# Second cross attention of a two-layer decoder: dense queries and 64-row score matmuls, one head per half of the rows and per bank

## The chip, the core and the metric

The kernel runs on one core of a Trainium2 chip. A core has five engines that run side by side and tell each other by semaphores how far they are: TensorE (PE: matmuls, with weight loads that the trace lists apart as PEld), VectorE (DVE), ScalarE (ACT), GpSimd (POOL) and SyncE (SP), which here issues the DMAs. Matmuls write to PSUM, eight banks of 128 partitions by 512 float32 numbers. The metric is the device time of one execution in microseconds. TensorE's clock is granted by a throttle at one of two levels; the traces show it as 1.00 (2.4 GHz) or 0.50 (1.2 GHz), or a mean of the two.

## The reference, cut to the stage of the change

Six sublayers follow each other, each with a residual and a layer norm: self attention, cross attention, experts, then the same three again in other forms. The change is in the fifth.

```python
def _L1_xattn_ref(query, context, w_q, w_kv, w_out, b_out):
    # NUM_HEADS 16, HEAD_DIM 64, B 8, 128 queries of width 128, 120 context rows of width 96
    q = query @ w_q
    kv = context @ w_kv
    k, v = jnp.split(kv, 2, axis=-1)
    q = q.reshape(B, NQ, NUM_HEADS, HEAD_DIM).transpose(0, 2, 1, 3)
    k = k.reshape(B, NKV, NUM_HEADS, HEAD_DIM).transpose(0, 2, 1, 3)
    v = v.reshape(B, NKV, NUM_HEADS, HEAD_DIM).transpose(0, 2, 1, 3)
    scores = jnp.einsum('bhqd,bhkd->bhqk', q, k) * SCALE
    attn = jax.nn.softmax(scores, axis=-1)
    out = jnp.einsum('bhqk,bhkd->bhqd', attn, v)
    out = out.transpose(0, 2, 1, 3).reshape(B, NQ, INNER)
    return out @ w_out + b_out

x = _layernorm(x + _L1_attn_ref(x, ...), axis=-1)
x = _layernorm(x + _L1_xattn_ref(x, ctx_768, ...), axis=-1)
x = _layernorm(x + _L1_ffn_ref(x, ...), axis=-1)
```

## The kernel before, in words

Every engine has its own program, written out in the order in which it runs; nothing is reordered by a scheduler, and the engines meet only at semaphores (`wait_ge`, `then_inc`).

The 16 heads are 64 wide, so two heads fill 128 partitions, and the stage works on 8 such pairs. The activations stand transposed in `xT` (128 features by 1024 tokens, 8 batches of 128), the context in `ctxT` (96 by 960, 8 batches of 120). For pair `n`, in the buffers of `slot` n modulo 2:

- TensorE projects the queries (`project_queries`, L872, two matmuls of 512 tokens into banks 0 and 1), ScalarE and VectorE copy them out and scale them. Head j = 0 of the pair lies in partitions 0 to 63, head 1 in 64 to 127. ScalarE copies partitions 0 to 63 and VectorE 64 to 127 into `qz`, which has two 128-column blocks a batch: in block 0 the partitions of head 1 are zero, in block 1 those of head 0. GpSimd writes these zeros once, with the memsets of L549 and L551, ahead of the stage.
- Keys (L880, copied by ScalarE into `kE`) and values (L888, copied by ScalarE into `vE`), in the same banks 0 and 1.
- Scores (`pair_scores`, L899): 16 matmuls of 128 rows by 120 columns, in four groups `g` of four. A group covers two batches and both heads, goes to one of two banks (2 and 3, in turn), and waits for VectorE to be through with the group two before it. The zeros in `qz` let a matmul over all 128 partitions give the scores of one head.
- VectorE takes a group's maximum (L1595) and subtracts it (L1597) into `probs`, ScalarE takes the exponential (`pair_exps`), VectorE sums and inverts (L1607, L1608), GpSimd multiplies (L559).
- TensorE transposes the probabilities (`pair_weights`, L909, four groups, banks 4 and 5 in turn), ScalarE copies each group into `ptE`; then come the value matmuls (`pair_values`, L922, 64 columns of the array for each head, banks 6 and 7, in two halves), copied into `otall`.

TensorE's step `n` (`pair_step`) does projections and scores of pair n + 1 and transposes and values of pair n, woven together. ScalarE's step has the order: query, key and value copies of pair n + 1, exponentials 0 and 1 of pair n + 1, copy of transpose group 0 of pair n, exponential 2, copy 1, exponential 3, copies 2 and 3, outputs. VectorE does queries, the four maxima and subtractions, then the four sums of one pair. The first pair's scores stand alone ahead of step 0; the loop runs over steps 2 to 5, and steps 0, 1, 6 and 7 are written out. After step 7 a projection (L971) ends the stage. A float32 matmul is two records of the trace (two loads and two matmuls), a transpose is one.

## Time and profile before

| | |
|---|---|
| median of 3 runs | 608.4 us (605.29 to 608.42) |
| profiled execution, span | 608.5 us |
| TensorE busy | 497.6 us (82%), 4128 records |
| weight loads busy | 359.7 us (59%) |
| VectorE, ScalarE, GpSimd busy | 295.4 (49%), 236.1 (39%), 124.7 us (20%) |
| mean granted TensorE clock | 0.897 |

Busy time is a share of the whole span, and the stages have different limits, so for a change in one stage one reads that stage: the timeline rows give the start and the duration of each instruction (or a run of equal ones, "x4"), and in brackets how long the engine had been idle before it and what released it. Matmuls are pipelined, and the end of the last of a run is modelled; the starts of the weight loads are the better marks of TensorE's pace.

### The profile page before, as it was taken

Reading aid. Unit: us, or ns where it says so; the run is one execution under the profiler, and the core shown is the slowest. Engines: PE = TensorE matmul, PEld = TensorE weight load, DVE = VectorE, ACT = ScalarE, POOL = GpSimd, SP = SyncE. Lnnn points to the kernel's source line nnn. Section 1 sums busy time; section 2 is a strip of 40 time slices with the busy share of each in tenths; the row PEclk is TensorE's granted clock in tenths of the full one; section 3 lists DMA queues with packets and bytes.
Section 4 is the critical chain, followed back from the end, with each engine's and each line's share of the span. In section 5 each row is a group of like instructions: output and inputs, shape, how many; then the busy total and the mean of one; then the engine's idle time right before and its main releaser. Section 6 shows DMA issues by size and latency. Waiting matters only on the chain.

```text
span 608.5 us, 11301 instructions
## 1 busy us (share of the span) xinstructions
PE 497.6 (82%) x4128; PEld 359.7 (59%) x4128; DVE 295.4 (49%) x693; ACT 236.1 (39%) x418; POOL 124.7 (20%) x232
## 2 busy tenths in 40 slices
PE   8466766666877899828889689999999899999994
PEld 3325555555655399415556447777778567777774
DVE  6944443444267543705443677667771234333325
ACT  2612333334523042301346335666663253333440
POOL 8501222222331005201121423222231100000001
PEclk9875777877998799985899889999999999999998
DMA  8643322221303000142220100000100011111110
GB/s 225 202 126 93 89 86 75 82 78 45 141 1 138 1 2 2 39 136 84 82 81 25 34 12 12 12 17 22 29 1 2 1 27 36 36 35 35 44 33 34
DMA packets 22334, 34.33 MB, mean 56 GB/s; under 512 B 6888, under 2 KB 15032, under 8 KB 22040
## 3 DMA queue, kind: packets, MB, share of 16 engines
q1 hardware_dynamic: 22296, 33.80, 18.4%
q8 instruction: 26, 0.43, 0.3%
q14 instruction: 12, 0.10, 0.1%
HBM read 28.26 MB, written 5.24 MB: 55 GB/s over the span
## 4 chain that ended last, share of the span: by engine, by line
PE 59%; DMA 18%; DVE 13%; ACT 3%; SPq 3%; issue 2%; POOL 1%; POOLq 0%; DVEq 0%; ACTq 0%
PE ps L1000 9%; PE ps L983 9%; DMA stq<-stackA 6%; DMA w1a<-stackA 5%; PE ps L899 4%; DMA w1a<-stackD 4%; PE ps L626 3%; PE ps L591 3%; PE ps L604 3%; PE ps L872 3%; PE ps L971 2%; PE ps L880 2%; PE ps L888 2%; PE ps L807 2%; SPq L335 2%
## 5 line engine op out<-in xcount | busy, mean ns | idle before, releaser
L1332 DVE TENSOR_REDUCE negm<-ps 128x4 f32<-128x512 f32 x96 | 63.7, 688 | 108.4 <-PE ps L591 105.4
L1048 ACT ACTIVATE probs<-ps 128x512 f32<-128x512 f32 (+1 forms) x100 | 56.4, 592 | 66.5 <-PE ps L604 65.7
L1670 DVE SCALAR_TENSOR_TENSOR racc<-ps,sm,racc 128x128 f32<-128x128 f32 x128 | 35.9, 344 | 63.2 <-PE ps L1000 63.1
L1048 ACT ACTIVATE arena<-ps,w1a 128x512 f32<-128x512 f32 x64 | 43.5, 687 | 58.9 <-PE ps L983 57.8
L1000 PEld LDWEIGHTS ps<-w1a,arena 128*128 128x128 f32 x512 | 59.4, 192 | 7.2 <-issue 6.2
L1000 PE MATMUL ps<-w1a,arena 128*128 128x128 f32 x512 | 59.8, 275 | 0.8 <-DVE racc L1661 0.8
L983 PE MATMUL ps<-xT,w1a 128*128 128x512 f32 x128 | 57.9, 594 | 1.4 <-ACT xT L1048 1.4
L1048 ACT ACTIVATE arena<-ps 128x512 f32<-128x512 f32 (+4 forms) x62 | 35.1, 574 | 43.8 <-PE ps L807 16.5
L559 POOL TENSOR_TENSOR probs<-probs,rzE 128x480 f32<-128x480 f32 x32 | 30.6, 988 | 76.0 <-DVE rzE L1608 76.0
L580 PE MATMUL ps<-onesb 128*128 128x512 bf16 x134 | 37.5, 439 | 9.3 <-ACT vall L1048 6.2
L591 PE MATMUL ps<-stk,stq 96*128 96x128 bf16 x192 | 23.2, 269 | 20.9 <-DMA stq<-stackA 20.1
L513 POOL TENSOR_SCALAR rstd<-mv 128x4 f32<-128x4 f32 x12 | 2.7, 228 | 177.4 <-DVE mv L1386 177.4
L591 PE MATMUL ps<-w1a 96*128 96x128 bf16 x192 | 22.4, 262 | 19.5 <-DMA w1a<-stackA 19.5
L983 PEld LDWEIGHTS ps<-xT,w1a 128*128 128x128 f32 x128 | 23.0, 190 | 24.4 <-issue 22.2
L899 PEld LDWEIGHTS ps<-arena 128*128 128x128 f32 x256 | 30.4, 192 | 7.9 <-ACT arena L1048 4.2
L899 PE MATMUL ps<-arena 128*128 128x120 f32 x256 | 33.2, 278 | 1.6 <-ACT arena L1048 0.8
L626 PE MATMUL ps<-probs,vs 128*32 128x128 f32 x768 | 33.8, 306 | 0.7 <-issue 0.7
L591 PEld LDWEIGHTS ps<-stk,stq 96*128 96x128 bf16 x192 | 16.8, 121 | 28.1 <-issue 17.5
L591 PEld LDWEIGHTS ps<-w1a 96*128 96x128 bf16 x192 | 16.4, 118 | 25.3 <-issue 12.4
L1595 DVE TENSOR_REDUCE negm<-ps 128x4 f32<-128x480 f32 x32 | 21.0, 655 | 20.8 <-PE ps L899 20.7
L588 PE MATMUL ps<-causS,identb 128*128 128x512 bf16 x32 | 15.3, 480 | 18.4 <-DMA stq<-stackD 14.6
L580 PEld LDWEIGHTS ps<-onesb 128*128 128x128 bf16 x134 | 14.4, 110 | 27.0 <-issue 7.2
(196 smaller groups left out, 865.6 us busy)
## 6 DMA issues: line engine op xcount, KB each, us to landing
w1a<-stackA SPq DMA_DIRECT2D x16, 288.0 KB
stackA<-arena SPq DMA_DIRECT2D x12, 256.0 KB, 2.8
stk<-stackA SPq DMA_DIRECT2D x8, 288.0 KB
stq<-stackA SPq DMA_DIRECT2D x8, 288.0 KB
w1a<-stackD SPq DMA_DIRECT2D x8, 288.0 KB
w1a<-in_w1a SPq DMA_DIRECT2D x1, 2048.0 KB, 7.5
w2a<-in_w2a SPq DMA_DIRECT2D x1, 2048.0 KB, 7.8
w1a<-in_w1b SPq DMA_DIRECT2D x16, 128.0 KB, 2.0
```

Of the source, the lines that this page charges most:

```text
L559: nc.gpsimd.tensor_tensor(weights, weights, along(rzE[:, slot, 4 * g:4 * g + 4], L), ALU.mult).then_inc(e_norm, 1)
L580: mm(bank(at), onesb[:], fill, start=True, stop=True)
L591: last = mm(o[:, k * P:(k + 1) * P], queries_of[slot][0:MROW, c, b * P:(b + 1) * P], keys_of[slot][0:MROW, c, b * P:(b + 1) * P], start=no ...
L604: last = mm(o[:, k * P:(k + 1) * P], keys_of[slot][0:MROW + PARTS, c, b * P:(b + 1) * P], queries_of[slot][0:MROW + PARTS, c, b * P:(b + 1 ...
L626: last = mm(bank(BANK_O + slot % 2)[32 * (b % 4):32 * (b % 4) + 32, col:col + P], vs[:, slot % 2, c if pair else 0, b, :], probs[:, slot % ...
L899: last = mm(bank(BANK_S + g % 2)[:, k * L:(k + 1) * L], qz[:, slot, b, j, :], kE[:, slot, b * L:(b + 1) * L], start=True, stop=True)
L983: mm(bank(BANK_S + u), w1s[:, slot, f * P:(f + 1) * P], xT[:, half * HALF:(half + 1) * HALF], start=True, stop=True).then_inc(g_up, 1)
L1000: last = mm(bank(banks + half)[:, k * P:(k + 1) * P], hid1[:, slot, f, b * P:(b + 1) * P], w2s[:, slot, f, :], start=f == 0, stop=f == F1 - 1)
L1048: return nc.scalar.activation(o, i, f, **kw)
L1332: nc.vector.tensor_reduce(negm[:, slot % 2, 4 * g:4 * g + 4], tiles(bank(BANK_S + g % 2), 4, P), AX.X, ALU.max, negate=True).then_inc(a.ma ...
L1595: nc.vector.tensor_reduce(negm[:, slot, 4 * g:4 * g + 4], s, AX.X, ALU.max).then_inc(e_max, 1)
L1670: last = stt(racc[:, b, :], bank(banks + half)[:, k * P:(k + 1) * P], sm[:, 11, bass.ds(b * E1 + e, 1)], racc[:, b, :], ALU.mult, ALU.add)
```

## The change

`qz` becomes `qE`, dense: both heads' queries of a token stand in one column, 128 partitions deep. ScalarE copies the first 512 tokens whole and VectorE the second, one copy each in place of two of 64 partitions. The memsets and their semaphore go. The key matmuls wait for one copy each. A score matmul takes the 64 partitions of its head alone from `qE` and `kE`; head 0 writes to bank 2 and head 1 to bank 3, in turns of one matmul. A half of the batches (`half`, eight matmuls) fills both banks and waits for VectorE to be through with both banks of the last half. `g` now counts half and head, not pairs of batches, and the value matmuls index `ptE` accordingly. TensorE's step has two score calls in place of four, the second behind the transpose groups 0 and 1. The orders of ScalarE, VectorE, GpSimd and SyncE in the steps stay. The diff, without the line that takes the semaphore `e_zero` from the list:

```diff
--- before.py
+++ after.py
@@ -182,7 +182,7 @@
         qB = area(0, B, P)
 
         otall = area(0, PAIRS, T)
-        qz = area(8192, 2, B, 2, P)
+        qE = area(8192, 2, T)
         kE = area(12288, 2, B * L)
         wE = area(14208, 2, 3, P)
 
@@ -546,10 +546,6 @@
             pool.wait_ge(D.lo, 2)
             pool.wait_ge(D.kept, 16 * 6)
             pool.wait_ge(ln_rstd, 8)
-            nc.gpsimd.memset(qz[0:64, :, :, 1, :], 0.0).then_inc(e_zero, 1)
-            pool.wait_ge(e_zero, 1)
-            nc.gpsimd.memset(qz[64:128, :, :, 0, :], 0.0).then_inc(e_zero, 1)
-            pool.wait_ge(e_zero, 2)
             add_bias(4, boE)
 
             def pair_norm(n, slot):
@@ -875,8 +871,7 @@
             def project_keys(n, slot):
                 for half in range(2):
                     if not early(n, 1):
-                        pe.wait_ge(e_qa, n * 2 + half + 1)
-                        pe.wait_ge(e_qd, n * 2 + half + 1)
+                        pe.wait_ge((e_qa, e_qd)[half], n + 1)
                     mm(bank(BANK_M0 + half)[:, 0:480], wE[0:CD, slot, 1, :], ctxT[:, half * 480:(half + 1) * 480],
                        start=True, stop=True).then_inc(e_k, 1)
 
@@ -889,16 +884,19 @@
                                   wE[0:CD, slot, 2, :], start=True, stop=True)
                     last.then_inc(e_v, 1)
 
-            def pair_scores(n, slot, g):
-
-                pe.wait_ge(e_kc, n * 2 + (2 if g >= 2 else 1))
-                if not early(4 * n + g, 2):
-                    pe.wait_ge(e_sub, n * 4 + g - 1)
+            def pair_scores(n, slot, half):
+
+                pe.wait_ge(e_kc, n * 2 + half + 1)
+                if half == 1 or not early(n, 1):
+                    pe.wait_ge(e_sub, n * 4 + 2 * half)
                 for k in range(4):
-                    b, j = 2 * g + k // 2, k % 2
-                    last = mm(bank(BANK_S + g % 2)[:, k * L:(k + 1) * L], qz[:, slot, b, j, :],
-                              kE[:, slot, b * L:(b + 1) * L], start=True, stop=True)
-                last.then_inc(e_s, 1)
+                    b = 4 * half + k
+                    for j in range(2):
+                        rows = slice(64 * j, 64 * j + 64)
+                        last = mm(bank(BANK_S + j)[:, k * L:(k + 1) * L], qE[rows, slot, b * P:(b + 1) * P],
+                                  kE[rows, slot, b * L:(b + 1) * L], start=True, stop=True)
+                        if k == 3:
+                            last.then_inc(e_s, 1)
 
             def pair_weights(n, slot, g):
 
@@ -920,7 +918,8 @@
                     for b in range(4 * half, 4 * half + 4):
                         for j in range(2):
                             last = mm(bank(BANK_O + half)[64 * j:64 * j + 64, b % 4 * P:(b % 4 + 1) * P],
-                                      vE[:, slot, b, 64 * j:64 * j + 64], ptE[:, slot, 2 * b + j, :], start=True, stop=True)
+                                      vE[:, slot, b, 64 * j:64 * j + 64], ptE[:, slot, 8 * half + 4 * j + b % 4, :],
+                                      start=True, stop=True)
                     last.then_inc(e_pv, 1)
 
             def pair_step(n, slot, turn, last=False):
@@ -933,12 +932,10 @@
                     project_queries(n + 1, 1 - slot)
                     project_keys(n + 1, 1 - slot)
                     pair_scores(n + 1, 1 - slot, 0)
+                    project_values(n + 1, 1 - slot)
+                    pair_weights(n, slot, 0)
+                    pair_weights(n, slot, 1)
                     pair_scores(n + 1, 1 - slot, 1)
-                    project_values(n + 1, 1 - slot)
-                    pair_scores(n + 1, 1 - slot, 2)
-                    pair_weights(n, slot, 0)
-                    pair_scores(n + 1, 1 - slot, 3)
-                    pair_weights(n, slot, 1)
                     pair_weights(n, slot, 2)
                     pair_weights(n, slot, 3)
                 pair_values(n, slot)
@@ -951,10 +948,10 @@
             to_feature(3)
             pe.wait_ge(ln_xT, 8)
             project_queries(0, 0)
-            pe.wait_ge(e_qa, 2)
-            pe.wait_ge(e_qd, 2)
-            for g in range(4):
-                pair_scores(0, 0, g)
+            pe.wait_ge(e_qa, 1)
+            pe.wait_ge(e_qd, 1)
+            for half in range(2):
+                pair_scores(0, 0, half)
             pair_step(0, 0, 1)
             pair_step(1, 1, 1)
             with pe.Fori(1, PAIRS // 2 - 1) as i:
@@ -1218,10 +1215,8 @@
 
             def copy_queries(n, slot):
 
-                for half in range(2):
-                    act.wait_ge(e_q, n * 2 + half + 1)
-                    fn(qz[0:64, slot, 4 * half:4 * half + 4, 0, :], tiles(bank(BANK_M0 + half)[0:64, :], 4, P),
-                       ACT.Copy, scale=XD ** -0.5).then_inc(e_qa, 1)
+                act.wait_ge(e_q, n * 2 + 1)
+                fn(qE[:, slot, 0:HALF], bank(BANK_M0), ACT.Copy, scale=XD ** -0.5).then_inc(e_qa, 1)
 
             def copy_keys_values(n, slot):
                 for half in range(2):
@@ -1273,7 +1268,8 @@
 
             copy_keys_values(0, 0)
             feature_copies(3)
-            act.wait_ge(e_zero, 2)
+            act.wait_ge(D.lo, 2)
+            act.wait_ge(D.kept, 16 * 6)
             copy_queries(0, 0)
             for g in range(4):
                 pair_exps(0, 0, g)
@@ -1580,10 +1576,8 @@
 
                 if not early(n, 2):
                     dve.wait_ge(e_s, 4 * (n - 1))
-                for half in range(2):
-                    dve.wait_ge(e_q, n * 2 + half + 1)
-                    ts(qz[64:P, slot, 4 * half:4 * half + 4, 1, :], tiles(bank(BANK_M0 + half)[64:P, :], 4, P), XD ** -0.5,
-                       None, ALU.mult).then_inc(e_qd, 1)
+                dve.wait_ge(e_q, n * 2 + 2)
+                ts(qE[:, slot, HALF:T], bank(BANK_M0 + 1), XD ** -0.5, None, ALU.mult).then_inc(e_qd, 1)
 
             def pair_maxima(n, slot):
 
@@ -1607,7 +1601,7 @@
                     link(nc.vector.tensor_reduce(r, probs[:, slot, 4 * g:4 * g + 4, 0:L], AX.X, ALU.add))
                     nc.vector.reciprocal(r, r).then_inc(e_rz, 1)
 
-            dve.wait_ge(e_zero, 2)
+            dve.wait_ge(D.kept, 16 * 6)
             pair_queries(0, 0)
             pair_maxima(0, 0)
             pair_queries(1, 1)
```

TensorE in the second written-out step: L888 (after: L883) are the value projections, L899 (L896) the scores, L909 (L907) the transposes. Before, from the value projections on:

```order
L888 MATMUL ps<-arena,ctxT 120x128 [waits e_kc]
L888 MATMUL ps<-arena,ctxT 120x128 x3
L888 MATMUL ps<-arena,ctxT 120x128 [waits e_kc]
L888 MATMUL ps<-arena,ctxT 120x128 x3
L899 MATMUL ps<-arena 128x120 [waits e_sub,e_kc]
L899 MATMUL ps<-arena 128x120 x3
L909 MATMUL ps<-con,probs 120x128 [waits e_ptc,e_norm]
L909 MATMUL ps<-con,probs 120x128 x3
L899 MATMUL ps<-arena 128x120 [waits e_sub,e_kc]
L899 MATMUL ps<-arena 128x120 x3
L909 MATMUL ps<-con,probs 120x128 [waits e_ptc,e_norm]
L909 MATMUL ps<-con,probs 120x128 x3
```

and after, from the first scores on:

```order
L896 MATMUL ps<-arena 128x120 [waits e_sub,e_kc]
L896 MATMUL ps<-arena 128x120 x7
L883 MATMUL ps<-arena,ctxT 120x128 [waits e_kc]
L883 MATMUL ps<-arena,ctxT 120x128 x3
L883 MATMUL ps<-arena,ctxT 120x128 [waits e_kc]
L883 MATMUL ps<-arena,ctxT 120x128 x3
L907 MATMUL ps<-con,probs 120x128 [waits e_ptc,e_norm]
L907 MATMUL ps<-con,probs 120x128 x3
L907 MATMUL ps<-con,probs 120x128 [waits e_ptc,e_norm]
L907 MATMUL ps<-con,probs 120x128 x3
L896 MATMUL ps<-arena 128x120 [waits e_sub,e_kc]
L896 MATMUL ps<-arena 128x120 x7
```

Eight transposes in place of four now stand ahead of the last scores, and groups 2 and 3 of the scores have become one run of eight behind one wait.

GpSimd ahead of the stage, from the second half of the layer norm's square root to the bias. Before:

```order
L513 TENSOR_SCALAR rstd<-mv 128x4 [waits ln_var]
L515 TENSOR_TENSOR rstd<-rstd,mhalf 128x4 [waits pchain]
L549 MEMSET arena 64x16x128 [waits ln_rstd,d_kept,d_lo]
L551 MEMSET arena 64x16x128 [waits e_zero]
L521 TENSOR_TENSOR xres<-xres,boE 128x1024 [waits ln_out,ln_xT,e_zero]
```

and after:

```order
L513 TENSOR_SCALAR rstd<-mv 128x4 [waits ln_var]
L515 TENSOR_TENSOR rstd<-rstd,mhalf 128x4 [waits pchain]
L521 TENSOR_TENSOR xres<-xres,boE 128x1024 [waits ln_xT,ln_rstd,ln_out,d_kept,d_lo]
L558 UNCONDITIONAL_BRANCH
L558 ISA
```

The two memsets are gone, and the bias addition waits for what they waited for.

## Rows read from the trace of the kernel before

**Rows 1.** Stretch view, one step: length, busy us (records) by engine, clock, DMA

```profile
core 0: us, PE busy (x) PEld busy (x) DVE busy (x) ACT busy (x) POOL busy (x), PEclk, DMA share, GB/s
415.15:429.00 13.85, 13.30 (x106) 10.03 (x104) 9.41 (x19) 8.85 (x16) 3.82 (x5) 1.00 0.19 50
```

**Rows 2.** Timeline, TensorE in that step: start us, us, engine, line

```profile
415.15 1.98 PE L872 MATMUL ps<-xT,arena 128*128 128x512 f32 x4
...
418.93 1.86 PEld L899 LDWEIGHTS ps<-arena 128*128 128x128 f32 x16 [0.65 <-issue]
...
422.45 0.97 PEld L899 LDWEIGHTS ps<-arena 128*128 128x128 f32 x8
...
426.23 0.41 PEld L909 LDWEIGHTS ps<-con,probs 128*120 128x120 f32 x4 [0.67 <-issue]
```

**Rows 3.** Timeline, VectorE in that step

```profile
420.12 0.66 DVE L1595 TENSOR_REDUCE negm<-ps 128x4 f32<-128x480 f32 x1 [2.25 <-PE ps L899]
...
422.06 0.66 DVE L1597 TENSOR_TENSOR probs<-ps,negm 128x480 f32<-128x480 f32 x1
423.64 0.66 DVE L1595 TENSOR_REDUCE negm<-ps 128x4 f32<-128x480 f32 x1 [0.92 <-PE ps L899]
...
425.66 0.66 DVE L1597 TENSOR_TENSOR probs<-ps,negm 128x480 f32<-128x480 f32 x1
```

**Rows 4.** Timeline, start of the stage

```profile
342.26 1.08 DVE L1396 TENSOR_SCALAR xres<-racc,mv,rstd 128x128 f32<-128x128 f32 x4
...
343.49 0.63 PE L713 MATMUL ps<-con,xres 128*128 128x128 f32 x4 [0.79 <-DVE xres L1396]
343.81 3.95 DVE L1396 TENSOR_SCALAR xres<-racc,mv,rstd 128x128 f32<-128x128 f32 x4 [0.47 <-POOL rstd L515]
343.92 1.80 POOL L549 MEMSET arena<- 64x2048 f32 x1
...
347.82 1.12 PE L713 MATMUL ps<-con,xres 128*128 128x128 f32 x4 [3.69 <-DVE xres L1396]
...
349.62 3.78 PE L872 MATMUL ps<-xT,arena 128*128 128x512 f32 x4 [0.69 <-ACT xT L1048]
```

**Rows 5.** Timeline, the first pair's scores

```profile
354.20 1.86 PEld L899 LDWEIGHTS ps<-arena 128*128 128x128 f32 x16 [2.38 <-ACT arena L1048]
...
355.39 0.66 DVE L1595 TENSOR_REDUCE negm<-ps 128x4 f32<-128x480 f32 x1 [1.26 <-PE ps L899]
356.09 0.66 DVE L1597 TENSOR_TENSOR probs<-ps,negm 128x480 f32<-128x480 f32 x1
...
356.86 0.97 PEld L899 LDWEIGHTS ps<-arena 128*128 128x128 f32 x8 [0.80 <-issue]
...
360.00 0.66 DVE L1597 TENSOR_TENSOR probs<-ps,negm 128x480 f32<-128x480 f32 x1
```

**Rows 6.** Groups by line, 400 to 520 us: busy us, mean ns | idle before

```profile
L1048 ACT ACTIVATE arena<-ps 128x512 f32 x8 | 4.8, 597 | 2.8 <-PE ps L922 2.3
L1048 ACT ACTIVATE arena<-ps 64x512 f32<-64x512 f32 x8 | 4.7, 591 | 2.5 <-PE ps L872 2.5
```

**Rows 7.** Stretch view of L922 over 10 ns; timeline of two runs of loads

```profile
412.96:412.97 0.01, 0.01 (x1) 0.01 (x2) 1.00 0.00 0
```

```profile
426.81 0.85 PEld L922 LDWEIGHTS ps<-w2a,w1a 120*64 120x64 f32 x16 [0.17 <-issue]
```

```profile
485.94 1.75 PEld L1011 LDWEIGHTS ps<-rw,xT 128*128 128x128 f32 x15 [0.24 <-issue]
```

**Rows 8.** Stretch view, TensorE alone: length, busy us (records), granted clock, DMA

```profile
143.50:144.50 1.00, 0.01 (x1) 1.00 0.62 242
...
145.00:145.50 0.50, 0.00 (x0) 0.57 0.33 107
```

```profile
298.50:299.00 0.50, 0.50 (x7) 0.67 0.46 188
...
301.50:302.50 1.00, 1.00 (x12) 0.71 0.19 78
```

```profile
346.00:346.50 0.50, 0.00 (x0) 0.96 0.00 0
```

More of the change, by code:

```diff
@@ L288, in decoder_kernel @@
         (e_q, e_k, e_v, e_qa, e_qd, e_kc, e_vc, e_s, e_max, e_sub, e_exp, e_rz, e_norm, e_pt, e_ptc, e_pv, e_oc,
-         e_zero, e_wo, e_y) = (
+         e_wo, e_y) = (
             sem("e_" + n) for n in ("q", "k", "v", "qa", "qd", "kc", "vc", "s", "max", "sub", "exp", "rz", "norm", "pt",
-                                    "ptc", "pv", "oc", "zero", "wo", "y"))
+                                    "ptc", "pv", "oc", "wo", "y"))
         woE = oT[:, 0:4, :, :].rearrange("p a b c -> p (a b) c")
```

## The prediction

> **What bounds the kernel now.** First I looked at the stretch view of the stage that the change touches, the second cross attention, which runs from about 359 to 462 us: seven steps of the same shape, each of which projects queries, keys and values of the next pair of heads and transposes and multiplies the probabilities of this one. One step takes 13.85 us with TensorE busy for 13.30, VectorE for 9.41, ScalarE for 8.85 [rows 1]. That looks like a TensorE bound, and would make every saved matmul time count. The order of time tells otherwise. In one step the scores' first weights load at 418.93, 3.78 us after the query projection began [rows 2]. VectorE's first maximum starts at 420.12, its second subtraction ends at 422.06 + 0.66 = 422.72, then it stands idle for 0.92 us, because the third group of scores is behind the value projection on TensorE; it goes on at 423.64 and ends the fourth subtraction at 425.66 + 0.66 = 426.32 [rows 3]. From there it is 2.68 us to the next step at 429.00: the last exponential, the last two copies of transposed probabilities on ScalarE, and the second half of the value matmuls. So a step is one chain in which TensorE, VectorE and ScalarE take turns: what counts is when VectorE gets its third group, not how much TensorE does.
>
> **The start of the stage.** GpSimd's two memsets go. The first ran from 343.92 for 1.80 us, the second right behind it, and the four layer norm instructions that VectorE had started at 343.81 took 3.95 us beside them, where the same four took 1.08 without them at 342.26 [rows 4]. Everything waits for these four: transposes, the copy, the query projection. Saved: 3.95 - 1.08 = 2.87 us. The transposes behind them took 1.12 us at the lower clock; the first half's took 0.63 [rows 4], since TensorE had idled and the granted clock fell in the slice from 346.0 [rows 8]. They now come at 345.0, ahead of that: another 0.45 saved, together **-3.3**. The query projection would begin at 346.3, just when the clock fell, with hardly any matmul before it, so I leave it at its slow 3.78 us; at full clock it takes 1.98 [rows 2, 4], and the bound on the good side is another -1.8.
>
> **The query copies.** Two copies of 64 partitions become one of 128 on each engine. A copy of 64x512 takes ScalarE 591 ns and one of 128x512 takes 597 [rows 6], so an engine saves one copy a step. The path does not: the first key matmul waits for the first half's copy as before, the second key matmul for VectorE's, which still follows the second query matmul. **0 us**; the engines' idle time covers it.
>
> **The scores' matmuls.** Each float32 matmul is two records. Eight records load their weights in 0.97 us, so one takes (0.97 - 0.19) / 7 = 0.111, and VectorE starts 1.19 us after the first load: 8 x 0.111 + 0.30 [rows 2, 3]. It is the load of 128 columns that sets this: with only 16 columns to stream, L1011 loads 15 records in 1.75 us, 0.111 again [rows 7]. The change keeps the number of records and of columns. It gains only where the two halves of the rows load and stream at the same time; no such matmul is in this trace. Upper bound of the cost: no overlap, 0.111 a record as now. Lower bound: full overlap, 0.111 for a pair, which is what L922 does with halves of the columns: two loads begin in the same 10 ns, and 16 records take 0.85 us [rows 7]. I take the lower bound, since L922 is the nearest row and its loads do start together. Eight matmuls then give VectorE both banks after 0.30 + 8 x 0.111 = 1.20 us; without overlap the first bank comes after 0.30 + 14 x 0.111 = 1.86.
> The Trainium skill speaks both ways. TensorEngine Tiling (Array Packing), Key Properties, says that different tiles can load weights and multiply in parallel; L922 agrees for column tiles. TensorE: Matmul & The Clock Gate, LDWEIGHTS, says that loading takes a time set by the columns and not by the rows, by which half the rows save nothing if loads take turns. By the first the step costs 0.40, by the second 1.72, as worked out below.
>
> **The order.** Here lies the cost. Before, group 2 was issued when the first bank was free, beside the value projection, and group 3 after it, so that VectorE found one bank while TensorE filled the other. Now the second half fills both banks at once and waits for the second subtraction. And it stands behind two transposes. VectorE's idle time becomes 0.11 (a subtraction that ended at 356.75 let scores load at 356.86 [rows 5]) + 1.20 = 1.31 us in place of 0.92. The step by this chain: 3.78 + 1.20 + 2.60 (two groups) + 0.11 + 1.20 + 2.68 (two groups) + 2.68 = 14.25, against 13.85: **+0.40**. Without overlap: 3.78 + 1.86 + 2.60 + 0.11 + 1.86 + 2.68 + 2.68 = 15.57, +1.72. TensorE is through with the values and transposes before the second subtraction ends, so that its order costs nothing more, and entering another tile shape falls into its wait. Seven steps: **+2.8**. The opening, where the first pair's scores stand alone, loses more: before it took 360.66 - 354.20 = 6.46 us from first load to last subtraction [rows 5], as VectorE never waited; now 1.20 + 2.60 + 0.11 + 1.20 + 2.68 = 7.79, **+1.3**.
>
> **What is queued behind the wait, and the clock.** ScalarE's order is unchanged: the copy of the second transpose group stands behind the third exponential, which waits for VectorE's third subtraction. TensorE's last transpose group needs that copy. Before, it loaded at 426.23 [rows 2], 1.24 us after the third subtraction ended (423.64 + 1.35), and its load side had been idle for 0.67. Now the third subtraction ends at 3.78 + 1.20 + 2.60 + 0.11 + 1.20 + 1.35 = 10.24 in the step, and the last group loads at 11.47; TensorE has loaded the scores' weights by 7.69 + 0.9 = 8.6, and with the third transpose group, which waits for one more copy, it is done by about 9.4. It idles some **2.1 us in the middle of every step**. In the steps before, the granted clock was 1.00, the 2.4 GHz level [rows 1]. But elsewhere it fell to 0.50 when TensorE had been idle for 1.6 us: nothing ran after 143.5, and a mean of 0.57 over the half microsecond from 145.0 puts the fall at 145.07 [rows 8]. One low stretch lasted from about 298.7 to 302.1, 3.4 us [rows 8]; the one that began in the slice from 346.0 covered the query projection until about 353.3, 6.8 us [rows 4, 8]. What follows the idle time is work on the chain: transposes, value matmuls, the next projections. 3.4 us at half the clock lose at most 1.7 there, 6.8 lose 3.4; some falls begin in the idle time and cost less. I take 1.5 us a fall, bounds 0 and 3.4, and a fall in six of seven steps: **+9.0**. In the opening TensorE idles still longer, 2.9 us between its two halves of scores, of which 16 records at half the clock cost another **+0.9**.
>
> **Sum.** -3.3 + 2.8 + 1.3 + 9.0 + 0.9 = +10.7 us on a span of 608.5. The median of the runs shown is 608.4 and the lowest 605.3, so the execution profiled stands at the median: 608.4 + 10.7 = 619.1.
>
> **Rivals.**
> 1. The clock holds. For it: the step keeps some 11 of 14 us of work on TensorE, and no row shows an idle time of 2.1 us between stretches as dense as these. Against: it is more than the 1.6 us after 143.5, and those followed a busy stretch too. Then -3.3 + 2.8 + 1.3 = +0.8: 609.2.
> 2. The halves' loads take turns, and the clock falls too. For it: the load sets the pace [rows 7], and no row shows two row halves. Opening: 1.86 + 2.60 + 0.11 + 1.86 + 2.68 = 9.11, +2.65; steps 7 x 1.72 = 12.0; start -3.3; clock 5 falls x 1.5 + 0.9 = 8.4: +19.8, 628.2. If the clock holds with it: +11.4, 619.8, which is in the forecast's own range.
> 3. The other side: the start outweighs the rest. Mechanism: without the memsets the query projection comes in time to keep the clock, -3.3 - 1.8 = -5.1, and the two halves deliver so early that VectorE's gap is the old 0.92 (both banks in 0.81 us rather than 1.20; it decides at 1.20 - 0.39). Then the opening costs +0.5 and the steps nothing, and the idle time is too short for the clock: -4.6, 603.8. Against it: nothing in the trace is quicker than 0.111 for a pair.
>
> **Numbers.** Chances: forecast 0.42, its own range 614 to 624; rival 2 with falls 0.22, without 0.08; rival 1 0.20; rival 3 0.08. A measurement of this kernel tells about 0.5% (3 us) from no change. Slower by more: 0.42 + 0.22 + 0.08 = 0.72; within: 0.20; faster: 0.08. The range goes from 607, under rival 1, to 629, over rival 2, and leaves out rival 3 and worse clocks.
>
> **What would show it.** Right: first two row-half loads beginning together and 16 records in about 0.9 us; VectorE idle for 1.3 us before its third maximum; TensorE idle for 2 us before the last transposes of a step, released by ScalarE's copy; a granted clock under 1.00 in most steps; steps of 15 to 16.5 us; the four layer norm instructions at 1.1 us. Wrong: steps of 14.3 us at full clock (rival 1), 16 records in 1.9 us (rival 2), or steps at or under 13.9 (rival 3).

## The result and the profile after

The changed kernel takes 615.0 us (median of 20 runs, 610.3 to 621.5) against 611.0 for the kernel before (20 runs, 605.0 to 616.4) on the same chip. The ratio, of the fast runs alone, is 1.0078, 95% interval 1.0049 to 1.0108: **slower by 0.8%**, 4.8 us (the medians of all runs differ by 4.0). The direction was forecast and the time lies in the range; the forecast of +10.7 us was more than twice too large.

The profiled execution after has a span of 609.3 us against 608.5; at 611.4 us it is the third quickest of the 20. From the second half of the layer norm (340.68, before 343.81) to the first load of the output projection (462.38, before 461.94) the stage took 121.70 us, before 118.13: +3.57. What stands ahead of the stage happened to be 3.1 us shorter in this execution; the change doesn't touch it.

The steps are counted here from 1 to 7, each from the query projection with which it begins; the transposes and values of the last pair stand behind those of step 7. Stretch view, first pair, then steps 1 to 4 and 7 with what follows it (the columns are those of [rows 1]):

```profile
343.19:351.97 8.78, 5.13 (x36) 3.49 (x36) 3.23 (x5) 1.80 (x3) 2.35 (x1) 0.78 0.06 19
351.97:369.49 17.52, 14.90 (x107) 10.28 (x105) 13.96 (x29) 8.87 (x16) 6.86 (x8) 0.82 0.04 10
369.49:384.52 15.03, 13.04 (x106) 9.16 (x104) 8.65 (x17) 8.26 (x15) 3.49 (x4) 0.93 0.04 12
384.52:399.25 14.73, 12.70 (x107) 8.68 (x105) 8.35 (x16) 8.26 (x15) 2.95 (x4) 0.96 0.04 12
399.25:413.40 14.15, 12.12 (x107) 8.39 (x105) 8.66 (x18) 8.27 (x15) 3.83 (x5) 1.00 0.05 13
...
441.69:462.38 20.69, 17.66 (x154) 13.30 (x152) 8.96 (x19) 12.26 (x23) 5.82 (x7) 0.92 0.01 2
```

Two kinds of step stand here. Steps 4 to 6 ran at full clock in 14.15 us, 0.30 over [rows 1]. In the others the granted clock is under 1.00. The same four stretches took 14.63, 13.79, 13.86 and 19.08 us in the kernel before, all at 1.00.

Timeline of TensorE's weight loads in a step at full clock, the answer to [rows 2] (L868 queries, L896 scores, L907 transposes):

```profile
413.40 0.30 PEld L868 LDWEIGHTS ps<-xT,arena 128*128 128x128 f32 x2 [0.17 <-issue]
...
417.17 0.97 PEld L896 LDWEIGHTS ps<-arena 64*128 64x128 f32 x16 [0.70 <-issue]
...
421.06 0.97 PEld L896 LDWEIGHTS ps<-arena 64*128 64x128 f32 x16 [0.17 <-DVE probs L1591]
422.48 0.41 PEld L907 LDWEIGHTS ps<-con,probs 128*120 128x120 f32 x4 [0.44 <-issue]
424.84 0.41 PEld L907 LDWEIGHTS ps<-con,probs 128*120 128x120 f32 x4 [1.95 <-issue]
```

The same step on VectorE, the answer to [rows 3], and on ScalarE (w2a are the copies of transposed weights):

```profile
418.35 0.66 DVE L1589 TENSOR_REDUCE negm<-ps 128x4 f32<-128x480 f32 x1 [2.24 <-PE ps L896]
...
420.30 0.66 DVE L1591 TENSOR_TENSOR probs<-ps,negm 128x480 f32<-128x480 f32 x1
422.25 0.66 DVE L1589 TENSOR_REDUCE negm<-ps 128x4 f32<-128x480 f32 x1 [1.29 <-PE ps L896]
...
424.20 0.66 DVE L1591 TENSOR_TENSOR probs<-ps,negm 128x480 f32<-128x480 f32 x1
```

```profile
423.64 0.60 ACT L1045 ACTIVATE probs<-probs 128x480 f32<-128x480 f32 x1 [1.27 <-DVE probs L1591]
424.14 0.58 ACT L1045 ACTIVATE w2a<-ps 120x512 f32<-120x512 f32 x1
```

The dense form does what was expected of it: 16 records load in 0.97 us where [rows 2] has 1.86. TensorE's work in a step falls from 13.30 to 12.12 us. But nothing is gained: the second lot of scores waits for the second subtraction, VectorE idles 1.29 us before its third maximum (0.92 in [rows 3]), and the last transposes begin to load after 1.95 us without a load. They waited for ScalarE's copy at 424.14, which stands behind the exponential of 423.64. Over the stage the view of waits has that as one line: engine and line waiting, releaser, us in all, times, longest.

```profile
PE ps L907 <- ACT w2a L1045: 14.4, 14, 2.0
```

Stretch view of TensorE beside such a wait in step 1, half microseconds:

```profile
364.50:365.00 0.50, 0.00 (x0) 0.00 (x0) 0.47 (x2) 0.50 (x2) 0.00 (x0) 1.00 0.00 0
365.00:365.50 0.50, 0.00 (x0) 0.00 (x0) 0.50 (x1) 0.47 (x1) 0.00 (x0) 0.74 0.00 0
...
368.50:369.00 0.50, 0.50 (x12) 0.50 (x10) 0.12 (x1) 0.36 (x1) 0.50 (x1) 0.85 0.00 0
```

The clock falls at about 365.2, in the idle time, and is back at about 368.7. The transposes and most of the value matmuls behind the wait run at the lower clock. In the other two falls it went down only when TensorE was at work again. In step 2 the last transposes ran from 380.97, and the clock fell at about 382.3, in the value matmuls:

```profile
380.97 0.63 PE L907 MATMUL ps<-con,probs 128*120 128x128 f32 x4 [1.75 <-ACT w2a L1045]
```

```profile
382.00:382.50 0.50, 0.50 (x12) 0.81 0.00 0
```

This low stretch lasted into step 3's query projection, until about 385.7. In step 7 the transposes ran from 453.18 and the clock fell at about 454.0.

Start of the stage, the answer to [rows 4], and the first pair's scores, the answer to [rows 5]:

```profile
340.68 1.11 DVE L1392 TENSOR_SCALAR xres<-racc,mv,rstd 128x128 f32<-128x128 f32 x4 [0.47 <-POOL rstd L515]
```

```profile
343.19 1.98 PE L868 MATMUL ps<-xT,arena 128*128 128x512 f32 x4 [0.69 <-ACT xT L1045]
```

```profile
346.04 1.00 PEld L896 LDWEIGHTS ps<-arena 64*128 64x128 f32 x16 [1.70 <-issue]
349.95 1.81 PEld L896 LDWEIGHTS ps<-arena 64*128 64x128 f32 x16 [2.91 <-issue]
```

The layer norm took 1.11 us in place of 3.95, and the query projection came 2.51 us behind its start, not 5.81. It ran at full clock here (1.98 us). The second lot of scores stood behind 2.9 us without a load and ran at the lower clock (1.81), as did the query projection of step 1 (3.47 us).

The +3.57 us in full, after less before, from one first load to the next:

| stretch | us |
|---|---|
| layer norm to first query projection | -3.30 |
| to the first scores | -1.73 |
| to the second query projection | +1.12 |
| step 1 | +2.89 |
| steps 2 and 3 | +2.11 |
| steps 4 to 6 | +0.87 |
| step 7 and its values | +1.61 |

### The profile page after: what moved, and what is told of

Same layout as the page of the kernel before. It is cut to its first block, busy times and chain, and to the rows that moved or that the text cites. A ratio compares the mean times of both kernels' runs of the same rounds, so it can differ in the third digit from the quotient of the medians.

```text
span 609.3 us, 11253 instructions
## 1 busy us (share of the span) xinstructions
PE 493.5 (81%) x4127; PEld 352.3 (58%) x4128; DVE 286.6 (47%) x685; ACT 231.5 (38%) x410; POOL 121.0 (20%) x230
## 4 chain that ended last, share of the span: by engine, by line
PE 59%; DMA 19%; DVE 13%; SPq 3%; ACT 2%; issue 2%; POOL 1%; POOLq 0%; DVEq 0%; ACTq 0%
PE ps L997 9%; PE ps L980 9%; DMA stq<-stackA 5%; DMA w1a<-stackA 5%; PE ps L920 3%; PE ps L622 3%; DMA stq<-stackD 3%; PE ps L587 3%; PE ps L896 3%; PE ps L868 3%; PE ps L600 3%; DMA w1a<-stackD 2%; PE ps L968 2%; PE ps L907 2%; PE ps L883 2%
## 5 line engine op out<-in xcount | busy, mean ns | idle before, releaser
L1045 ACT ACTIVATE arena<-ps 128x512 f32<-128x512 f32 (+3 forms) x54 | 30.5, 573 | 48.7 <-PE ps L803 15.9
L576 PE MATMUL ps<-onesb 128*128 128x512 bf16 x134 | 36.2, 428 | 6.0 <-ACT vall L1045 2.9
L907 PE MATMUL ps<-con,probs 128*120 128x128 f32 x128 | 18.8, 281 | 14.4 <-ACT w2a L1045 14.4
L587 PEld LDWEIGHTS ps<-w1a 96*128 96x128 bf16 x192 | 15.6, 115 | 23.7 <-DMA w1a<-stackA 10.9
L1045 ACT ACTIVATE probs<-probs 128x480 f32<-128x480 f32 x34 | 19.7, 599 | 23.7 <-DVE probs L1591 18.2
```

Of the source, the lines that this page charges most:

```text
L576: mm(bank(at), onesb[:], fill, start=True, stop=True)
L587: last = mm(o[:, k * P:(k + 1) * P], queries_of[slot][0:MROW, c, b * P:(b + 1) * P], keys_of[slot][0:MROW, c, b * P:(b + 1) * P], start=no ...
L907: last = nc.tensor.transpose(bank(BANK_T + g % 2)[0:L, k * P:(k + 1) * P], probs[:, slot, 4 * g + k, 0:L], ident)
L1045: return nc.scalar.activation(o, i, f, **kw)
```

## Experiments

Each ratio is to runs of the kernel before taken beside it, with its 95% interval; experiments 1 to 4 ran on one chip, 5 to 8 on another. A step's length is that of the profiled execution.

**1. Weave the scores again.** The second half's scores are split by head and put where groups 2 and 3 stood before; head 0's wait for the first subtraction alone. The first pair's second half is split too.

```
-                    pair_weights(n, slot, 0)
-                    pair_weights(n, slot, 1)
-                    pair_scores(n + 1, 1 - slot, 1)
+                    pair_scores(n + 1, 1 - slot, 1, (0,))
+                    pair_weights(n, slot, 0)
+                    pair_scores(n + 1, 1 - slot, 1, (1,))
+                    pair_weights(n, slot, 1)
```

> Dense queries and 64-row matmuls as in the change, but the second half's scores go back to two groups of four, one head and one bank each: head 0's waits for VectorE's first subtraction and stands behind the value projection, head 1's waits for the second and stands behind the first transposes, as before the change. Theory (the cost of the change is the one wait for both banks and what stands behind it): VectorE's gap before the third maximum goes, since the projections are 0.9 us earlier and the third group's scores (8 x 0.111 + 0.30 us) are there when the second subtraction ends; step 3.78 + 1.20 + 4 x 1.31 + 2.7 = 12.9 us against 14.15 at full clock after the change and 13.85 before; TensorE idles under 1 us before its last transposes, and the granted clock stays 1.00 in the steps. Stage about 10 us shorter than before (118.1), kernel 1.5% faster than before. Rival (what costs is the 64-row matmuls themselves or the change of tile shape): the step stays at 14 us or more, since there are now three changes of shape more.

Measured: ratio to before 0.9965 (0.993 to 1.000), where 0.985 was expected. Steps 2 to 6 take 13.68 us at a granted clock of 1.00, so weaving takes back 0.47 of the 14.15. Loads of a step:

```profile
400.33 0.96 PEld L896 LDWEIGHTS ps<-arena 64*128 64x128 f32 x8
401.41 0.41 PEld L907 LDWEIGHTS ps<-con,probs 128*120 128x120 f32 x4
401.99 0.96 PEld L896 LDWEIGHTS ps<-arena 64*128 64x128 f32 x8 [0.17 <-issue]
```

The 12.9 us were missed, and the stage is 0.8 us shorter than before, not 10. A group of one head alone loads 8 records in 0.96 us, as slowly as 128 rows (0.97 for 8 in [rows 2]): the saving is there only where the heads alternate. And the loads stand one behind the other without a wait: TensorE's own order now sets when VectorE gets its third and fourth group. The 0.47 is thus what the order gives back less what these slower loads take.

**2. The start alone.** The kernel before, with the two memsets moved ahead on GpSimd, out of the way of the layer norm; nothing else.

```
             heads(D, PAIRS, 8)
-            rsqrt(3, 0)
-            rsqrt(3, 1)
             pool.wait_ge(D.lo, 2)
             pool.wait_ge(D.kept, 16 * 6)
-            pool.wait_ge(ln_rstd, 8)
             nc.gpsimd.memset(qz[0:64, :, :, 1, :], 0.0).then_inc(e_zero, 1)
             pool.wait_ge(e_zero, 1)
             nc.gpsimd.memset(qz[64:128, :, :, 0, :], 0.0).then_inc(e_zero, 1)
             pool.wait_ge(e_zero, 2)
+            rsqrt(3, 0)
+            rsqrt(3, 1)
+            pool.wait_ge(ln_rstd, 8)
```

> The kernel before with its two memsets issued ahead of the layer norm's square roots rather than behind them; nothing else differs. Theory (memsets beside VectorE's layer norm cost 2.9 us, and the idle TensorE's clock 1.8 more): the four layer norm instructions take 1.1 us and not 3.95, first scores 5.0 us after them and not 10.4, kernel 3 to 5 us faster (0.5 to 0.8%). Rival (the start is hidden or the clock falls anyway): 0 to 3 us.

Measured: 0.9961 (0.9923 to 0.9999), some 2.4 us faster, less than the 3 to 5 expected. VectorE and TensorE's first scores:

```profile
341.29 1.11 DVE L1396 TENSOR_SCALAR xres<-racc,mv,rstd 128x128 f32<-128x128 f32 x4 [0.46 <-POOL rstd L515]
```

```profile
348.39 6.24 PEld L899 LDWEIGHTS ps<-arena 128*128 128x128 f32 x32 [2.38 <-ACT arena L1048]
```

The memsets did stretch the layer norm. But of the 3.30 us won to the query projection the stage kept 1.72 (116.41 against 118.13). The scores, which in the kernel before began 10.39 us behind the layer norm's start and at full clock (1.86 us for 16 records in [rows 5]), began after 7.10 (5.0 was expected), while the clock was still low: 32 records took 6.24. The rival, by which the clock falls anyway, came true.

**3. Fill TensorE's idle time.** The changed kernel with 12 matmuls that nobody reads between the first pair's two lots of scores, and 8 before the last transposes of each step.

```
             pair_scores(0, 0, 0)
+            keep_busy(12, BANK_M0)
             pair_scores(0, 0, 1)
...
                     pair_weights(n, slot, 2)
+                    pe.wait_ge(e_vc, (n + 1) * 2 + 2)
+                    keep_busy(8, BANK_M0)
                     pair_weights(n, slot, 3)
```

> The changed kernel with matmuls on ones that nobody reads, while TensorE waits: 12 between the two halves of the first pair's scores, 8 ahead of the last transposes of each step. Theory (TensorE's idle 2 us lower the clock in some of the steps, about 1.5 us each time): granted clock 1.00 over the whole stage, all steps 14.15 us, opening 0.9 us shorter; stage 3 to 5 us shorter than after the change (121.7). Rival (the low clock falls on waits and costs nothing, or 8 x 0.22 us of filling delays the last transposes): same time or slower.

Measured: 1.0073 (1.0042 to 1.0104), no better than the changed kernel; the stage, expected 3 to 5 us shorter, is 2.1 longer in the profiled execution (123.8). Stretch view from the middle of its step 3 to the end of the stage, and the twelve extra matmuls in the opening:

```profile
394.00:463.00 69.00, 66.82 (x570) 45.04 (x568) 40.88 (x82) 42.12 (x77) 19.10 (x20) 1.00 0.06 15
```

```profile
348.99 3.82 PE L576 MATMUL ps<-onesb 128*128 128x512 bf16 x12
```

Steps 2 to 6 take 14.15 or 14.16 us at a granted clock of 1.00, and step 7 with what follows 19.44, not 20.69. So with the gap filled no clock fell in them, and 14.15 is the step without falls; what steps 2, 3 and 7 of the changed kernel exceed it by is what its falls cost. This is one execution, and the changed kernel too kept the clock in four of its seven gaps: that filling is what held it is likely, not shown. The gain was lost in the opening, where the query projection ran at the lower clock (3.78 us) and the twelve matmuls after it took 3.82: the second lot of scores came 5.75 us behind the first, not 3.91. Step 1 took 19.32 us, not 17.52, with a clock of 0.50 from about 358.0 to 364.8.

**4. One head after the other.** The changed kernel with all four score matmuls of head 0 ahead of those of head 1.

```
-                for k in range(4):
-                    b = 4 * half + k
-                    for j in range(2):
+                for j in range(2):
+                    for k in range(4):
+                        b = 4 * half + k
```

> The changed kernel with the score matmuls of a half in another order: four of head 0, then four of head 1, so that neighbours use the same half of the rows and cannot overlap. Theory (the chain needs only the first bank at once, and the time to it is the same): 16 records in 1.8 us and not 1.0, but VectorE's first maximum 1.2 us after the first load as with overlap, gap before the third maximum 1.3, step 14.15 to 14.3 us at full clock: the overlap is worth nothing in this order. Rival (overlap is what keeps the change near the old time): first maximum 1.9 us after the first load, step 15.5 us, kernel 1.5% slower than the change.

Measured: 1.0179 (1.0116 to 1.0242). Loads and VectorE in a step:

```profile
391.12 1.51 PEld L896 LDWEIGHTS ps<-arena 64*128 64x128 f32 x16 [0.71 <-issue]
...
395.56 1.51 PEld L896 LDWEIGHTS ps<-arena 64*128 64x128 f32 x16 [0.17 <-issue]
```

```profile
396.75 0.66 DVE L1589 TENSOR_REDUCE negm<-ps 128x4 f32<-128x480 f32 x1 [1.83 <-PE ps L896]
```

Order alone makes 1.51 us of 0.97. VectorE's gap grows from 1.29 to 1.83 and the step from 14.15 to 14.69, by 0.54, the same as the loads' growth. Both expectations missed: VectorE has its first bank 1.19 us after the first load, as the theory said, but the longer loads delay all that stands behind them on TensorE, and the second lot now starts 0.64 us after the second subtraction and not 0.10. Steps 3 and 5 took 16.08, with a clock fall (1.39 us each), steps 2, 4 and 6 14.69. The alternation of row halves is what the dense form lives from.

**5. Mend ScalarE's queue.** The changed kernel with the four copies of transposed weights ahead of the third and fourth exponential.

```
                     pair_exps(n + 1, 1 - slot, 1)
-                    pair_weights(n, slot, 0)
-                    pair_exps(n + 1, 1 - slot, 2)
-                    pair_weights(n, slot, 1)
-                    pair_exps(n + 1, 1 - slot, 3)
-                    pair_weights(n, slot, 2)
-                    pair_weights(n, slot, 3)
+                    for g in range(4):
+                        pair_weights(n, slot, g)
+                    pair_exps(n + 1, 1 - slot, 2)
+                    pair_exps(n + 1, 1 - slot, 3)
```

> The changed kernel with one edit on ScalarE: the copies of all four groups of transposed weights stand ahead of the third and the fourth exponential of the next pair, in place of between and behind them. Theory (the step of the changed kernel ends on ScalarE's second copy, which is queued behind the third exponential, which waits for TensorE's late second scores; TensorE idles 2 us there): the second copy then runs at once behind the first, the last transposes follow the third group without a wait, and the 2.0 us of idle go. A steady step is what TensorE works in one: 14.15 - 1.85 = 12.3 to 12.6 us; no clock falls behind the start; 7 steps are 14.15 to 12.5, -11 us, and the falls (some 3.5 us) go too: 615.0 - 14 = 601 us. Rival (what the dense form saved was never on the path; something else, the exponentials or the sums, ends the step as late as before): the idle moves to the next projection or the next transposes, step 13.9 to 14.15, 612 to 615 us.

Measured: 602.6 us (5 runs), 0.9874 (0.9828 to 0.992): 1.3% faster than the kernel before and, by the two ratios, 2% faster than the changed one. Stretch view of steps 4 and 5, then TensorE and ScalarE in step 5:

```profile
390.88:403.81 12.93, 11.88 (x106) 8.41 (x105) 8.66 (x17) 8.05 (x17) 3.82 (x4) 1.00 0.05 14
403.81:416.33 12.52, 11.88 (x106) 8.41 (x104) 8.66 (x17) 8.04 (x17) 3.82 (x4) 1.00 0.17 45
```

```profile
413.40 1.11 PE L907 MATMUL ps<-con,probs 128*120 128x128 f32 x8 [0.29 <-ACT w2a L1045]
414.44 1.97 PE L920 MATMUL ps<-w2a,w1a 120*64 120x128 f32 x32
```

```profile
414.06 1.09 ACT L1045 ACTIVATE w2a<-ps 120x512 f32<-120x512 f32 x2 [0.32 <-PE ps L907]
415.04 1.34 ACT L1045 ACTIVATE probs<-probs 128x480 f32<-128x480 f32 x2
```

Both last transpose groups run in one go, the wait before them is 0.29 us, and the exponentials that held the copies now follow them. Steps fell to 12.5 to 12.9 us at full clock; the stage took 111.0 us against 121.7. TensorE is busy for 11.88 of them. The largest wait left (0.3 to 0.8 us a step) was the second key matmul's for VectorE's query copy, which stands behind the row sums.

**6. The same edit on the kernel before.** Its ScalarE step has the same lines.

```
                     pair_exps(n + 1, 1 - slot, 1)
-                    pair_weights(n, slot, 0)
+                    for g in range(4):
+                        pair_weights(n, slot, g)
                     pair_exps(n + 1, 1 - slot, 2)
-                    pair_weights(n, slot, 1)
                     pair_exps(n + 1, 1 - slot, 3)
-                    pair_weights(n, slot, 2)
-                    pair_weights(n, slot, 3)
```

> The kernel before (128-row score matmuls with zeros) with the same edit on ScalarE: all four copies of transposed weights ahead of the third and fourth exponential. Theory: TensorE waits only 0.46 us for a copy in a step of the kernel before, so it gains at most that: step 13.86 to 13.4 to 13.6, 7 steps -2 to -3 us, 605.5 us. With the run of the changed kernel under the same edit this gives what the dense form is worth once its step no longer ends on the copy: about 1.0 us a step by theory (two lots of 16 records at 0.97 us in place of 1.86 would be 1.8, less the changes of tile shape). Rival (the edit itself is what helps, dense or not): both kernels gain as much, and the changed one stays slower by 0.8%.

Measured: 0.9963 (0.9921 to 1.0006). Two of its steps:

```profile
384.50:397.95 13.45, 13.09 (x106) 10.05 (x104) 9.53 (x18) 8.63 (x17) 3.82 (x5) 1.00 0.05 13
397.95:411.66 13.71, 13.09 (x106) 10.13 (x104) 9.45 (x18) 8.68 (x17) 3.83 (x5) 1.00 0.05 13
```

It won 0.3 us a step; TensorE is busy for 13.09 of some 13.6 and has no more to give. The changed kernel won 1.3 by the same edit. With ScalarE's queue mended the change is worth 0.9874 / 0.9963 = 0.991, about 0.9% faster (0.3 to 1.5% as an estimate from the two intervals), where without it the change cost 0.8%. In both, TensorE's work is by then near the length of a step.

**7. The order without the dense form.** The kernel before, its zeros and 128-row matmuls kept, with the order of the change on TensorE.

```
-                    project_values(n + 1, 1 - slot)
-                    pair_scores(n + 1, 1 - slot, 2)
-                    pair_weights(n, slot, 0)
-                    pair_scores(n + 1, 1 - slot, 3)
-                    pair_weights(n, slot, 1)
+                    project_values(n + 1, 1 - slot)
+                    pair_weights(n, slot, 0)
+                    pair_weights(n, slot, 1)
+                    pair_scores(n + 1, 1 - slot, 2)
+                    pair_scores(n + 1, 1 - slot, 3)
```

> The kernel before with the order of the change alone: values of the next pair behind its first scores, the first two groups of transposes next, and both second groups of scores behind them; the matmuls stay 128 rows deep with zeros. It is the change undone in its form and kept in its order. Theory (the order delays the third scores, the dense form gives part of it back): the third scores end at about +9.45 us of the step, third maximum and subtraction till +10.9, exponential and copy till +12.1, transposes and values till +14.95: step 15.0 us at full clock against 13.86 before and 14.15 after, with a clock fall in most steps as TensorE idles 1.5 us; 608 + 7 x 1.1 + some falls = 616 to 622 us. Rival (the order costs nothing and the dense form itself is what costs, by changes of tile shape): step 13.9, 608 us.

Measured: 1.0124 (1.0075 to 1.0174), 3 runs. Loads of a step, then VectorE and TensorE:

```profile
413.21 1.87 PEld L899 LDWEIGHTS ps<-arena 128*128 128x128 f32 x16
```

```profile
414.41 0.66 DVE L1595 TENSOR_REDUCE negm<-ps 128x4 f32<-128x480 f32 x1 [1.80 <-PE ps L899]
```

```profile
417.03 0.63 PE L909 MATMUL ps<-con,probs 128*120 128x128 f32 x4 [1.32 <-ACT w2a L1048]
```

Steps 3 to 6 take 14.67 us, and all seven have a granted clock of 1.00, with TensorE idle for 1.32 us in each. So **the order costs 0.81 us a step, and the dense form gives 0.52 back** (14.67 to 14.15): the +0.30 is a sum of two larger terms. Of the 0.3 by which the 15.0 expected was too much, 0.2 lie ahead of the third subtraction, which ended at +10.7 and not +10.9. The falls expected with it did not come.

**8. The memsets put back.** The changed kernel with both memsets, and the waits for them, where they were. Nothing reads the zeros.

```
             pool.wait_ge(ln_rstd, 8)
+            nc.gpsimd.memset(qz[0:64, :, :, 1, :], 0.0).then_inc(e_zero, 1)
+            pool.wait_ge(e_zero, 1)
+            nc.gpsimd.memset(qz[64:128, :, :, 0, :], 0.0).then_inc(e_zero, 1)
+            pool.wait_ge(e_zero, 2)
             add_bias(4, boE)
...
-            act.wait_ge(D.lo, 2)
-            act.wait_ge(D.kept, 16 * 6)
+            act.wait_ge(e_zero, 2)
...
-            dve.wait_ge(D.kept, 16 * 6)
+            dve.wait_ge(e_zero, 2)
```

> The changed kernel with GpSimd's two memsets put back at the start of the stage, and the waits for them; nothing reads the zeros. It is the start of the change undone alone. Theory (the start gives 3 us or more back, and the steps lose it): from the layer norm's second half to the first query projection 5.8 us again in place of 2.5; steps and the first pair's scores as in the changed kernel; +3.3 to +5 us, 618 to 620 us. Rival (the start was hidden, as by the clock, which is low through the scores when they come early): within 1 us of the changed kernel.

Measured: 1.0153 (1.0098 to 1.0208), 3 runs: by the two ratios 0.75% or 4.6 us over the changed kernel (0.1 to 1.4% as an estimate from the two intervals). Start of the stage:

```profile
344.08 3.95 DVE L1396 TENSOR_SCALAR xres<-racc,mv,rstd 128x128 f32<-128x128 f32 x4 [0.46 <-POOL rstd L516]
```

```profile
354.54 1.82 PEld L901 LDWEIGHTS ps<-arena 64*128 64x128 f32 x16 [2.45 <-issue]
359.36 1.81 PEld L901 LDWEIGHTS ps<-arena 64*128 64x128 f32 x16 [3.00 <-issue]
```

Layer norm to query projection is 5.80 us again (+3.29). The clock, low from 348 on, stayed low through both lots of scores until about 365; with padded scores [rows 5] it had been back when they began. So the start of the change is worth what was taken for it, 3.3 us. The stage is 6.3 us longer than the changed kernel's, 3.3 of it the layer norm and 2.7 the stretch from the first query projection to the second (11.50 against 8.78). That the memsets cost these 2.7 too is not shown: experiments 1 and 4, without them, took 11.46 and 11.18 there. The steps repeat those of the changed kernel: falls in 1, 2 and 7 and none in 3 to 6.

## Why the prediction was right or wrong

**The bound of the kernel before** was read rightly: a chain in turns and not TensorE. Experiments 6 and 7 show both sides of it.

**Overlap of the row halves.** Right. Two loads side by side from [rows 7] gave 0.9 us for 16 records; 0.97 was measured, and VectorE started 1.18 us after the first load (1.20 forecast). The row it rested on had column halves; row halves do the same, if they alternate (experiment 4). By the Trainium skill, TensorEngine Tiling (Array Packing), Key Properties, different tiles can load weights and multiply in parallel, and the 0.97 agrees. By the Trainium skill, TensorE: Matmul & The Clock Gate, LDWEIGHTS, the columns and not the rows set the time of a load, and 0.96 us for 8 records of one half alone (experiment 1), against 0.97 for 8 of 128 rows, agrees. The two rules do not exclude each other: each load is as long as before, but two run side by side.

**The step.** Forecast 14.25, measured 14.15. The chain read from the trace after is 3.77 + 1.18 + 2.61 + 0.10 + 1.19 + 2.61 + 2.69; only the third and fourth group were a little cheaper than the 2.68 taken. Its cause was named rightly as the order, though its size, 0.81 with 0.52 back, only shows in experiment 7. Seven steps cost +2.1 by this, not +2.8.

**The start.** -3.3 forecast, -3.30 measured to the query projection. That the projection stays at the lower clock was wrong for this execution (1.98 us, another -1.73) and right for the profiled runs of experiments 1, 3, 4 and 5 (3.4 to 3.8 us). They start the same way but take 10.5 to 11.5 us from the first query projection to the second (experiment 3 with its twelve extra matmuls), against 8.78. So the profile after is probably a lucky one there, and it is the medians (+4.8 us), not its +3.57, that should be compared. What decides this clock was not settled.

**The opening.** Right. Forecast +1.3 and +0.9; from first load to last subtraction it took 8.62 us against 6.46, +2.16. TensorE's next query projection doesn't wait for the last subtraction and came only 1.12 later. The other 1.04 stand in step 1, whose first maximum came 7.14 us after its query projection began, before 6.16. Step 1 has one thing more that the sum left out: in the kernel before VectorE was late there and waited only 0.50 us before its third maximum, not 0.92, so the new order cost 0.4 more in this step.

**The clock falls: the step that failed.** The term of +9.0 us failed, by its count. The wait was as described: TensorE idle before the last transposes (1.74 us by its matmuls, 2.1 forecast), released by ScalarE's copy. The price was about right: steps 2 and 3, which share a fall, lost 0.88 + 0.58 = 1.46 us and step 7 lost 1.61 - 0.30 = 1.31. In step 1 it was 1.2: from its first maximum to the next query projection 10.38 us passed, in a step at full clock 9.20. Taken was 1.5. But the argument took every gap over 1.6 us for a fall, six of seven steps, from the one idle stretch at 143.5 [rows 8], and there were falls in three steps: 1, 2 and 7. Step 7 fell after a gap of 1.74 us, and steps 3 to 6 kept the clock through one of 1.74. In experiment 4 the gap is 1.52 in each of steps 2 to 6 and two of them have a fall; in experiment 7, with 1.32, none has. Nor does the clock always fall in the gap: in steps 2 and 7 it fell 1.3 and 0.8 us behind its end. What picks the gaps that are followed by a fall stays open.

With three falls and 4.0 us in place of 9.0, the forecast becomes +5.7. The query projection at full clock (1.7), 0.1 us a step (0.7) and the 0.4 of step 1 bring it to +3.7, and the trace has +3.57.

**Where luck came in.** The forecast was added to 608.4, the median of three runs; twenty runs of the same kernel have 611.0. With the +4.8 measured on 608.4 the time would have been 613.2, under the 614 to 624 of the forecast's own range, though within 607 to 629. That 615.0 lies inside the narrower one is owed to the base.

**The rivals.** Rival 2 (loads take turns) is out by 0.97 us. Rival 1 (the clock holds) was half true: it held in four of seven gaps, and steps 4 to 6 took 14.15. Rival 3 had the early start's -5.1 as this execution shows it (-3.30 - 1.73), but VectorE's gap stayed 1.29, so it did not decide.

**What was missed.** The queue behind the wait was named as a cause of idle time and clock falls. It was not followed one question further: what the step would be with ScalarE's copies ahead of the exponentials. Experiment 5 answers it: 12.5 to 12.9.

## What to carry to other kernels

Work taken off an engine pays only if the chain that ends each step runs through it; here 1.2 us a step came off TensorE and the step grew, until an in-order queue on another engine (a copy behind an exponential that waits) was turned round, and then the same saving paid about 0.9%. When matmuls are merged into fewer, larger calls, look at what they delay downstream and reorder every engine's queue with them. Idle time like the 1.7 us here, inside a dense loop, is worth its own term for the clock, as a chance for each gap and not as a certainty.

## What the hardware showed that was not expected

- Float32 matmuls on 64 rows: 16 records in 0.97 us where two row halves alternate, 1.51 where eight records of one half are followed by eight of the other, and 0.96 for 8 alone, no faster than 128 rows.
- The granted clock fell to half in step 7 and held in steps 3 to 6 with the same instructions and the same gap of 1.74 us before the last transposes, in one execution; in experiment 4, with 1.52 us of idle time in each, it fell in every second step (14.69, 16.08, 14.69, 16.08).
- A fall need not come in the idle time. In step 2 TensorE had worked for 1.3 us again, in step 7 for 0.8, when the clock went down.
- How long a low stretch lasts at the start of the stage differs with little cause to be seen: in experiment 8 the clock was low from 348 to about 365 us, through both lots of scores; in the kernel before, with the same memsets, it was back at 353.3, ahead of them. That is one profiled execution each, and its cause was not tried.
